# The first expert's value product in three passes of split operands, in a two-layer mixture-of-experts kernel

## The reference

```python
weights = top2(softmax(t @ gate_w.T))                 # two of eight experts a token
h1 = t @ w1.T + 2 * (t @ a1[e]) @ b1[e]               # rank 16 an expert
h3 = t @ w3.T + 2 * (t @ a3[e]) @ b3[e]
act = silu(h1) * h3                                   # 512 features, for each of the two experts
out = sum over e of weights[e] * (act @ w2 + 2 * (act @ a2[e]) @ b2[e])
```

## Time and profile before

| what | us |
|---|---|
| runs | 974.18, 970.34, 972.42; median 972.42 |
| profiled execution | 970.89 |
| its span, first to last instruction | 969.1 |
| PE busy | 919.5 |
| POOL busy | 592.3 |

### The profile page before, as it was taken

The page is one execution under the profiler, slowest core; times in us unless marked ns, Lnnn a source line. Parts: engine busy times, 40 slices in busy tenths (PEclk is TensorE's granted clock), DMA queues, the critical chain, the costliest instruction groups (busy, mean ns, idle before and its releaser), DMA issues. The chain is left out here.

```text
span 969.1 us, 17609 instructions
## 1 busy us (share of the span) xinstructions
PE 919.5 (95%) x5060; PEld 698.9 (72%) x5067; DVE 685.0 (71%) x2098; ACT 555.7 (57%) x1255; POOL 592.3 (61%) x565
## 2 busy tenths in 40 slices
PE   6999999999999999999999999889998999989996
PEld 3777777777777767777767776568994676658996
DVE  5657678888888797888898787474542567665553
ACT  4444655766757577674664443135663676635663
POOL 5678868868577586776867876544441244552443
PEclk8899999999999999999999999999999999999999
DMA  6890000000000000000000000435544000005552
GB/s 182 356 404 2 1 1 1 1 1 1 1 1 1 1 1 1 2 0 1 12 1 12 13 1 27 146 105 179 180 148 119 2 13 23 24 32 152 179 178 87
DMA packets 39774, 62.74 MB, mean 65 GB/s; under 512 B 7073, under 2 KB 23266, under 8 KB 37504
## 3 DMA queue, kind: packets, MB, share of 16 engines
q1 hardware_dynamic: 35136, 53.08, 16.7%
q0 software_dynamic: 4544, 8.54, 2.6%
HBM read 34.68 MB, written 27.82 MB: 64 GB/s over the span
## 5 line engine op out<-in xcount | busy, mean ns | idle before, releaser
L384 PE MATMUL bank<-split 128*128 128x512 f32 x544 | 244.0, 448 | 5.8 <-POOL split L1816 3.0
L386 PE MATMUL bank<-split 128*128 128x512 f32 x544 | 214.9, 395 | 0.0
L385 PE MATMUL bank<-split 128*128 128x512 f32 x544 | 213.8, 393 | 0.0
L909 ACT ACTIVATE sil<-bank 128x512 f32<-128x512 f32 x128 | 76.0, 594 | 147.2 <-PE bank L386 146.7
L384 PEld LDWEIGHTS bank<-split 128*128 128x128 f32 x544 | 103.0, 189 | 36.0 <-issue 10.4
L385 PEld LDWEIGHTS bank<-split 128*128 128x128 f32 x544 | 103.4, 190 | 26.3 <-issue 10.5
L1295 DVE TENSOR_TENSOR act<-bank,sil 128x512 f32<-128x512 f32 x128 | 87.7, 685 | 48.3 <-PE bank L386 25.4
L386 PEld LDWEIGHTS bank<-split 128*128 128x128 f32 x544 | 102.9, 189 | 23.8
L1772 POOL TENSOR_TENSOR act<-act 128x512 f32<-128x512 f32 x64 | 88.6, 1384 | 27.9 <-DVE act L1301 27.7
L1778 POOL TENSOR_TENSOR split<-act,split 128x512 fp32r<-128x512 f32 x64 | 89.7, 1403 | 16.5 <-ACT split L976 16.2
L735 PE MATMUL bank<-xlT,e 128*128 128x128 f32 x624 | 84.2, 278 | 7.8 <-ACT hT_e L1172 4.5
(11 more groups left out here) (314 smaller groups left out, 2010.7 us busy)
## 6 DMA issues: line engine op xcount, KB each, us to landing
e<-e_dram SPq DMA_DIRECT2D x78, 256.0 KB
rows_in<-yw SPq DMA_DIRECT2D x17, 1056.0 KB, 17.9
xin<-rows_in SPq DMA_DIRECT2D x78, 66.0 KB
e<-e_dram SPq DMA_DIRECT2D x4, 512.0 KB, 7.9
x<-rows_out SPq DMA_DIRECT2D x8, 256.0 KB, 4.6
rows_in<-yw,slot_i POOLq DMA_INDIRECT x64, 2.3
rows_out<-ob,ids POOLq DMA_INDIRECT x39
out<-ob,ids POOLq DMA_INDIRECT x39
```

The costliest lines, as they stand in the source:

```text
L384: mm(dst, w[0], m[0], start=start, stop=False, **more)
L385: mm(dst, w[0], m[1], start=False, stop=False, **more)
L386: return mm(dst, w[1], m[0], start=False, stop=stop, **more)
L909: af(sil[(k - 1) % 2][:, :], bank[BH1[STEPS[k - 1][0] % 2]][:, :], ACT.Silu).then_inc(silu_done.sem, 1)
```

## The change

`value` uses `mm3`: the first expert's activations `act0[j]` are split into `firsts[j]`, the high part by a new copy on ACT (`first_high_of`), the low part by a new subtraction on POOL (`first_low_of`); for blocks 0 and 1 the low part is written over `act0[j]` itself, after `total(j)` has read it. `ua` and `ud` become two sets (for odd and even chunks), placed where their low parts go, so that the subtraction writes over its input; DVE's wait ahead of writing them changes from the low parts of the chunk before to the products of the chunk before that. The split buffer grows from 43 to 53 blocks, other tensors move, and some semaphores are merged (`prod_saved` and `eb2_steps` into `late_made`, `tanh_done` into `slot_w`).

```diff
# PE, value
+                        if g == 0:
+                            pe.wait_ge(weight_rest.sem, len(LOW_POOL) + 2)
                     for j in js:
-                        pe.wait_ge(*act_done(g, STEP[j, 0]))
-                        last = mm(bank[BV][:, :], a2[:, j, :], act0[j][:, :], start=j == 0, stop=j == J - 1)
+                        pe.wait_ge(*first_low(g, j + 1))
+                        last = mm3(bank[BV][:, :], tuple(w[:, rows(j)] for w in a2s), firsts[j], j == 0, j == J - 1)
# ACT
+                def first_high_of(j):
+                    if g is None:
+                        return
+                    act.wait_ge(*act_done(g, STEP[j, 0]))
+                    act.wait_ge(*v_ready(g - 1, 1))
+                    af(firsts[j][0], act0[j][:, :], ACT.Copy).then_inc(first_high.sem, 1)
...
                 a_high()
+                first_high_of(0)
+                first_high_of(1)
                 silu(3)
...
                 mask(1)
+                first_high_of(2)
                 silu(6)
...
                 a_mid(1)
+                first_high_of(3)
                 a_gate(1)
# DVE, masked(i)
-                    dve.wait_ge(*u_low(q - 1))
-                    v.tensor_tensor(ua[i][:, :], u_bank(q, i)[:, :], mT0[:, :], ALU.mult).then_inc(u_masked.sem, 1)
+                    dve.wait_ge(*h3_ready(q - 2))
+                    v.tensor_tensor(ua[p][i], u_bank(q, i)[:, :], mT0[:, :], ALU.mult).then_inc(u_masked.sem, 1)
...
             tables(0)
+            dve.wait_ge(late_made.sem, 4)
             bias_parts()
-            dve.wait_ge(prod_saved.sem, 4)
# POOL
+                def first_low_of(j):
+                    if g is None:
+                        return
+                    pool.wait_ge(*first_high(g, j + 1))
+                    if j < 2:
+                        pool.wait_ge(*summed(g, j + 1))
+                    pool.tensor_tensor(out=firsts[j][1], in0=act0[j][:, :], in1=firsts[j][0].bitcast(F32), op=ALU.subtract
+                                       ).then_inc(first_low.sem, 1)
...
                 total(1)
+                first_low_of(0)
                 sums_low(g, 0)
                 mask_diff()
                 sums_low(g, 1)
                 f_scale()
                 a_scale()
                 r_scale(s.r_stat)
+                first_low_of(1)
+                first_low_of(2)
+                first_low_of(3)
                 up_low(q, 0, 0)
                 total(2)
```

More of the change, by code:

```diff
@@ L159, in build @@
         yn_l = [yn_f, yn_a]
-        zT, pr_, pT = mT1, act0[0:2], act0[2:4]
         vu = [z, h2]
         nb_l = sb("nb_l", [P, T]); nmx = sb("nmx", [P, 2]); rs = sb("rs", [P, 2]); rsi = sb("rsi", [P, T])
-        with nc.sbuf_tensor("split", [P, 43 * S], F32R) as split:
+        with nc.sbuf_tensor("split", [P, 53 * S], F32R) as split:
             def part(n):
@@ L169, in parts @@
                 return part(n), part(n + 1)
[L171 to L178, removed]
+            w1s, w3s, b1s, b3s = (parts(17 + 2 * i) for i in range(4))
+            a1s, a3s = (tuple(split[:, 25 * S + (k + i) * P:25 * S + (k + i + 1) * P] for k in range(2)) for i in (0, 2))
+            ts = [parts(26), parts(28)]
+            uas, uds = ([[(part(30 + 4 * p + 2 * k + i), part(9 + 4 * p + 2 * k + i)) for i in range(2)] for p in range(2)] for k in range(2))
+            gs = [(part(38 + j), part(j)) for j in range(J)]
+            w2s, a2s = parts(42), parts(44)
+            hTs = part(46), part(4)
+            firsts = [(part(47 + j), part((5, 6, 51, 52)[j])) for j in range(J)]
         act1 = [sb(f"act1{j}", [P, S]) for j in range(J)]
+        hT = sb("hT", [P, S])
+        act0 = [sb(f"act0{j}", [P, S]) for j in range(J)]
         act_ = [act0, act1]
-        hT = sb("hT", [P, S])
+        with nc.sbuf_tensor("masked_u", [P, 8 * S], F32) as masked_u:
+            ua, ud = ([[masked_u[:, (4 * p + 2 * k + i) * S:(4 * p + 2 * k + i + 1) * S] for i in range(2)] for p in range(2)] for k in range(2))
+        w1, w3, b1, b3 = act0
+        zT, pr_, pT = mT1, act0[0:2], act0[2:4]
         yT = [tT, hT]
@@ L865, in _ @@
             keep_busy(9)
-            pe.wait_ge(*eb2_steps(0))
+            pe.wait_ge(late_made.sem, 10)
             pe.wait_ge(e2_loaded.sem, 16 * len(e2_loads))
@@ L893, in products @@
                 act.wait_ge(prod_ready.sem, 2)
-                af(wak[:, :], bank[0][:, 0:P], ACT.Copy).then_inc(prod_saved.sem, 1)
-                af(wuT[:, :], bank[1][:, 0:P], ACT.Copy).then_inc(prod_saved.sem, 1)
+                af(wak[:, :], bank[0][:, 0:P], ACT.Copy).then_inc(late_made.sem, 1)
+                af(wuT[:, :], bank[1][:, 0:P], ACT.Copy).then_inc(late_made.sem, 1)
                 act.wait_ge(prod_ready.sem, 3)
-                af(eb1T[:, :, :].rearrange("p e j -> p (e j)"), bank[3][:, 0:E * J], ACT.Copy).then_inc(prod_saved.sem, 1)
+                af(eb1T[:, :, :].rearrange("p e j -> p (e j)"), bank[3][:, 0:E * J], ACT.Copy).then_inc(late_made.sem, 1)
                 act.wait_ge(prod_ready.sem, 4)
-                af(gmat[:, :], bank[2][:, 0:P], ACT.Copy).then_inc(prod_saved.sem, 1)
+                af(gmat[:, :], bank[2][:, 0:P], ACT.Copy).then_inc(late_made.sem, 1)
             def first_layer(s):
@@ L941, in slot_weights @@
                     act.wait_ge(*maskT_ready(q - 1))
-                    af(th[:, :], dlt[:, :], ACT.Tanh, scale=0.5).then_inc(tanh_done.sem, 1)
-                    act.wait_ge(*tanh_done(q))
+                    af(th[:, :], dlt[:, :], ACT.Tanh, scale=0.5).then_inc(slot_w.sem, 1)
+                    act.wait_ge(*slot_w(q, 1))
                     act.wait_ge(*xf_done(q - 3))
@@ L981, in up_high @@
                     act.wait_ge(*h3_ready(q - 2))
-                    for k, (dst, src) in enumerate(((uas[q % 2][i][0], ua[i]), (uds[q % 2][i][0], ud[i]))):
+                    for k, (dst, src) in enumerate(((uas[q % 2][i][0], ua[q % 2][i]), (uds[q % 2][i][0], ud[q % 2][i]))):
                         act.wait_ge(*u_masked(q, 2 * i + k + 1))
@@ L1245, in _ @@
             products()
-            act.wait_ge(prod_saved.sem, 4)
+            act.wait_ge(late_made.sem, 4)
             tiles(0, 2, expert)
@@ L1305, in slot_ratio @@
                         return
-                    dve.wait_ge(*slot_w(q, 1))
+                    dve.wait_ge(*slot_w(q, 2))
                     v.reciprocal(wts[:, :], half_w[q % 3][:, :]).then_inc(slot_w.sem, 1)
@@ L1632, in chain @@
                 def chain(ins, n):
-                    ins.then_inc(eb2_steps.sem, 1)
-                    dve.wait_ge(*eb2_steps(0, n))
+                    ins.then_inc(late_made.sem, 1)
+                    dve.wait_ge(late_made.sem, 4 + n)
                 dve.wait_ge(late_loaded.sem, 16 * len(late_loads))
@@ L1815, in up_low @@
                     pool.wait_ge(*u_high(n, 2 * i + k + 1))
-                    pool.tensor_tensor(out=dst[n % 2][i][1], in0=src[i][:, :], in1=dst[n % 2][i][0].bitcast(F32), op=ALU.subtract
+                    pool.tensor_tensor(out=dst[n % 2][i][1], in0=src[n % 2][i], in1=dst[n % 2][i][0].bitcast(F32), op=ALU.subtract
                                        ).then_inc(u_low.sem, 1)
```

25 lines of the change are left out of this document (10 added, 15 removed).

## The result

The changed kernel takes 1000.22 us (median of 6 runs, 997.06 to 1005.26) beside 971.87 of the kernel before on the same chip: a ratio of 1.030, 95% interval 1.028 to 1.032. The sign was forecast, the size was not: +28 us in place of +8, and outside the range.

A forecast was written before the change was run, and what follows sets the result against it. PE was taken to bound the first layer, with POOL what PE waits for in slots 13 to 15. Terms -4.95 + 2.8 + 0.3 + 9.9 = +8.1 us on 970.9 gave 979.0, said as 980.5 for the median; range 969 to 987.

The forecast's parts named there:

- The base sum: All slots: PE's gains against POOL's delays, -4.95 + 2.8 + 0.3 + 9.9 = +8.1 us.
- slot 0: First slot: POOL is idle 2.65 us at the place, so it gives another 0.6 us of gain.
- slots 1, 2 and value of 3: Early slots: POOL idle only 0.64 us in slots 1 and 2, costing 1.4 each, +2.8; slot 3 gains 0.68.
- The lock: Five POOL-bound slots: DVE operations and POOL subtractions exclude each other, 7.4 us at most, likely 985; rival, chance 0.11.
- Slots 3 to 10: ... PE does not notice: Subtractions fit POOL's idle 2.40 to 4.64 us or delay `up_low` 1 to 1.4; slots gain 4.35 us.
- Slots 11 and 12: POOL idle 1.9 and 2.2 us: later `up_low` costs h(3,1) about what `value` gave, +0.3 us for both.
- Slots 13 to 15: Last slots: PE already waits for POOL, so three subtractions delay each by 3.4, 3.4 and 3.1 us, +9.9.
- the tests that the prediction named: Profile after: PE waits at `value` in slots 1, 2, 13, 14, 15; `lora_out` waits 1 us or more in 13 to 15.
- the sign that it is wrong: Slots 13 to 15 show no PE wait behind POOL, or slots 3 to 10 grow instead of shrinking.
- Everything hidden: All slots: POOL's lateness never reaches PE, each slot keeps 0.68 us, 961.5 us; rival, chance 0.13.
- the drain absorbs: End of the slots: slot 15 and part of slot 14 cost nothing, 975.7 us; rival, chance 0.14.

The follow-up runs named there:

- v_after: Changed kernel with the second expert's SiLU product written back to its PSUM bank and the weighting reading it there, complete: 982.66 us, ratio 1.011.
- v_before: Kernel before with the second expert's SiLU product written back to its PSUM bank and the weighting reading it there, complete: 967.65 us, ratio 0.997.
- the memsets: Two runs of the changed kernel with each subtraction replaced by a POOL memset that reads nothing: shorter row 981.40 us, longer row 992.10 us.
- x_none: Changed kernel without copies and subtractions, `value` back to four f32 products; two sets, semaphores and memory places kept: 969.55 us, ratio 0.998.
- y_1_11_14: Changed kernel with three passes in slots 1, 11 and 14 alone, f32 products in the others: 978.21 us, ratio 1.008.
- y_early: Changed kernel with three of the four subtractions moved to earlier places on POOL, only the last staying ahead of `up_low`: 990.73 us, ratio 1.021.
- x_34: Changed kernel with three passes in slots 3 and 4 only, f32 products in the others: 976.79 us, ratio 1.006.
- x_nolow: Changed kernel with the copies and twelve split matmuls but no subtraction, so the output lacks that correction: 966.99 us, ratio 0.996.
- z_dve: Changed kernel with all four subtractions on DVE: 986.56 us, ratio 1.016.
- z_mix: Changed kernel with two subtractions on POOL behind the totals and two on DVE: 990.77 us, ratio 1.019.
- w_after: Changed kernel with the second expert's weighting reading its first operand from PSUM, SiLU factor left out: 982.70 us.
- x_5to10: Changed kernel with three passes in slots 5 to 10 only, f32 products in the other ten: 970.69 us, ratio 1.000.
- y_dummy: Changed kernel with copies and subtractions kept but `value` in f32, so nothing on PE waits for the new work itself: 993.91 us, ratio 1.024.
- w_before: Kernel before with the second expert's weighting reading its first operand from PSUM, SiLU factor left out: 967.91 us.
- v_5to10: Changed kernel with the second expert's activation left in PSUM, and three passes in slots 5 to 10 alone: 965.88 us, ratio 0.995.

## Why the prediction was wrong, step by step

**The base sum was nearly right.** Set against the pair in which the weighting reads PSUM, the prediction's groups come out as follows (us, up to the first expert tile, from the periods of the traces; the prediction's slot 0, -0.6, lies ahead of the first period):

```
group                                   predicted   change   v_after - v_before
slots 1, 2 and value of 3                    +2.1     +5.6         +3.0
values of 4 to 10                            -3.7     +2.6         -2.9
11 to 15 and the way to the first tile      +10.2    +16.1        +10.6
```

The mechanism that the forecast described, POOL's in-order queue with a row of three ahead of `up_low`, no slack in the last slots and 0.68 of gain where there is slack, is there, and its sums hold to about 1 us a group. In part that is luck. In the middle group slots 4 and 5, given 0.68 each, came out at +0.46 and -0.07, while slots 8 and 10, given nothing and 0.27, gained 0.70 and 0.67. In the last group up to 1.7 of the 10.6 goes with a granted clock of 0.57 from 612 to 616 us in `v_after`, where `v_before` has 1.00. And the pair still differs by 15.0 us in its medians and not by 8.1; most of the rest lies behind the first tile (below).

**The step that failed is "The lock".** The prediction gave it 7.4 us at most and a chance of 0.11, in five slots, and argued that what DVE runs at that place "stays two". The count did stay. But before, POOL was idle beside the third of a slot's four weightings, the first at that place, in 11 of the 16 slots; the new row stands beside this weighting or the next in all of them. The part that goes with the weighting's second memory operand is 28.4 - 15.0 = 13.4 us. It is in three places: the row itself (4.25 in place of 3.75 us, at the 11 us for each microsecond of the memsets some 6, an estimate), the instructions behind it, and DVE, whose weighting takes 1055 ns in the mean after, 939 before and 691 from PSUM. The prediction counted POOL's delay only, and only where POOL was already the bound.

**"Slots 3 to 10: ... PE does not notice" failed in slots 3 and 4.** The lateness of `up_low` was to be 1 to 1.4 us. It was 3.6 in slot 4: 1.35 by the queue, 0.5 by the stretched row, and 1.8 because `up_low` (0,0), total 2 and `up_low` (0,1) slid beside the weighting and DVE's scans. PE had slack for some 1.5 of it and waited 2.1. In the pair with PSUM the two periods are +0.46 and -0.07: the gain is gone there too, and in one half a microsecond more.

**Slots 11 and 12** were +0.3 and lost more in the change (+2.56 in the period of slot 12 alone). The prediction let the lateness of `up_low` cost about what `value` gave. In that period PE waits for `up_low` twice, 0.81 and 1.10 us, where it did not wait before, and 0.38 longer for DVE; a small routing instruction of DVE, shown in the last section, has a part in the last.

**Slots 13 to 15** were right: +9.9 forecast, and slot 14 alone measured 3.39 against 3.4. Of the tests that the prediction named, PE's waits at `value` came in the five slots listed (and 0.27 and 0.26 us in slots 0 and 11), and `lora_out` waited in slots 13 and 14 (1.38, 0.64, and not 1 or more in both); behind slot 15 it no longer waits, and the wait stands one step earlier, at the sums' low part (2.71, 0.88 before). POOL's idle time in slot 7 fell from 4.64 to 0.42, where 0.9 was said. Of slots 5 to 8, said to be 0.65 shorter, only 7 and 8 were. Slots 3 to 6 grew, which the prediction itself gave as the sign that it is wrong.

**Outside the sum** are the 2.1 us behind the first tile; 6.1 in the profiled `v_after` against `v_before`. The change adds no work to that part, the semaphores that it merges there stand in `x_none` too, which has 328.2 us, and the runs don't settle the cause.

**The rivals.** "Everything hidden" and "the drain absorbs" found no support: the way from the last value to the first tile grew by 3.2. What the change would cost without collisions is best read from the memsets, about 12 us by the slope, and there the sum of 8.1 is 4 us low.

## What to carry to other kernels

When work is added to POOL, look at what DVE runs beside the new place, not only at how long POOL was idle there: here an instruction of DVE with two operands in memory and one of POOL that reads memory held each other up (1.34 in place of 0.69 us, 1.73 in place of 1.28), and both engines' queues behind them paid. Before moving work, see whether DVE's partner can read an operand from PSUM: here that made the kernel before 0.3% faster by itself and took half of the change's loss away. Where a queue has slots of different kinds, apply a change slot by slot: of sixteen, six could carry it, with a gain too small to be sure of.

## What was not expected of the hardware

**A DVE instruction can wait for more than one of POOL's operations.** In slot 12 of the changed kernel DVE's comparison of 128x32 elements (L1556) takes 3.24 us, and 3.22 in `y_1_11_14`. It ends with the second of two POOL operations that follow a scatter without a gap:

```profile
492.44 0.16 DVE L1555 TENSOR_TENSOR ala<-mx,inv 128x4 f32<-128x4 f32 x1
492.52 3.24 DVE L1556 TENSOR_TENSOR gt<-lg,mx 128x32 f32<-128x32 f32 x1
495.79 0.19 DVE L1557 TENSOR_TENSOR pr<-gt,pri 128x32 f32<-128x32 f32 x1
```

```profile
491.90 1.24 POOL L1945 DMA_INDIRECT rows_in<-yw,slot_i  x1 [0.30 <-issue]
493.17 1.31 POOL L1813 TENSOR_TENSOR r<-r 128x512 f32<-128x512 f32 x1
494.43 1.27 POOL L1784 TENSOR_TENSOR act<-act 128x512 f32<-128x512 f32 x1
```

Before, the same instruction took 0.18:

```profile
485.28 0.18 DVE L1544 TENSOR_TENSOR gt<-lg,mx 128x32 f32<-128x32 f32 x1
```

There DVE's weighting ahead of it took 2.21 us, and `total`, which waits for it, started 0.64 us behind `values`. So the wait moved more than it grew: from the activation ahead of these instructions to the one behind them DVE takes 5.55 us, and took 5.10 before. That POOL's operations stand back to back is not the whole reason: in `y_early`, shown above, each of the first two waiting instructions ended with a single operation of POOL, although POOL's next had started 0.04 us before that operation ended. What decides between the two is not shown.

**Two waits of PE of the same length had different consequences for its clock.** In `x_34` a wait of 2.11 us ahead of 150.60 and one of 2.10 ahead of 190.22 were followed by the lower level, a granted clock of 0.59 from 150 to 154 and of 0.50 from 192 to 196; in the changed kernel, 2.07 us ahead of 194.87, it stayed at 1.00. Busy time by stretches, `x_34` first (the third number from the end is the clock):

```profile
150.00:154.00 4.00, 3.40 (x10) 2.81 (x11) 0.76 (x2) 2.11 (x4) 4.00 (x4) 0.59 0.00 0
188.00:192.00 4.00, 1.90 (x10) 1.56 (x10) 2.37 (x3) 2.84 (x6) 4.00 (x4) 0.96 0.00 0
192.00:196.00 4.00, 4.00 (x15) 3.44 (x15) 0.39 (x2) 2.67 (x7) 4.00 (x4) 0.50 0.01 2
196.00:200.00 4.00, 4.00 (x16) 2.97 (x15) 1.84 (x5) 0.72 (x2) 4.00 (x4) 0.69 0.01 4
```

```profile
192.00:196.00 4.00, 1.93 (x11) 1.28 (x11) 2.41 (x3) 2.30 (x5) 4.00 (x3) 1.00 0.00 0
196.00:200.00 4.00, 4.00 (x25) 3.46 (x24) 1.99 (x6) 3.61 (x8) 4.00 (x5) 1.00 0.02 4
```

**The part behind the first tile was longer in the profiled execution of every kernel with split values in all slots**: 329.5 to 333.7 us in nine (the change, `x_nolow`, `y_early`, both memsets, `z_dve`, `z_mix`, `w_after`, `v_after`), and 326.2 to 329.2 in nine with f32 values in ten slots or more (before, `x_none`, `x_5to10`, `x_34`, `y_dummy`, `y_1_11_14`, `w_before`, `v_before`, `v_5to10`). At their nearest the two groups are 0.3 us apart, with one execution of each kernel. In the three longest, `x_nolow`, `z_mix` and `v_after`, PE stands for 1.8 to 2.4 us at a tile's first matmul without a wait that the profile shows, and the clock then falls (0.82 from 650 to 655 us in `x_nolow`, 0.66 from 666 to 671 in `v_after`). The cause was not tried.
